# Last attention of a four-layer network: plain float32 products, a later turn of the probabilities, output tiles spread over units

## What is computed

```python
x = _rmsnorm(hidden_states, ln_w)
q = jnp.einsum('bqd,hd->bqh', x, wq).reshape(B, Qlen, N_HEADS, HEAD_DIM)
k = jnp.einsum('bkd,hd->bkh', encoder_hidden_states, wk).reshape(B, Klen, N_KV_HEADS, HEAD_DIM)
v = jnp.einsum('bkd,hd->bkh', encoder_hidden_states, wv).reshape(B, Klen, N_KV_HEADS, HEAD_DIM)
...
scores = jnp.einsum('bhqd,bhkd->bhqk', q, k) / np.sqrt(HEAD_DIM).astype(np.float32)
attn = jax.nn.softmax(scores.astype(jnp.float32), axis=-1).astype(q.dtype)
out = jnp.einsum('bhqk,bhkd->bhqd', attn, v)
return jnp.einsum('bqh,dh->bqd', out, wo)
```

## Time and profile before

| | |
|---|---|
| median of 3 runs | 1754.61 us (1748.97 to 1754.72) |
| profiled execution, its own time | 1750.64 us |
| span in the profile | 1748.9 us |
| busy: PE, PEld | 1451.7 us (83%), 1150.0 us (66%) |
| busy: DVE, ACT, POOL | 1115.7 us (64%), 461.4 us (26%), 312.8 us (18%) |
| chain that ended last, shares | PE 62%, DVE 26%, ACT 4%, issue 4%, DMA 2% |

### The profile page before, as it was taken

How to read it: one execution, slowest core, us unless ns; L and a number is a source line. 1 busy time by engine, 2 the same in 40 slices (tenths; PEclk the granted TensorE clock), 3 DMA queues, 4 the chain that set the end, 5 groups by cost and what they waited for, 6 DMA issues and landing times.

```text
span 1748.9 us, 19188 instructions
## 1 busy us (share of the span) xinstructions
PE 1451.7 (83%) x6585; PEld 1150.0 (66%) x6585; DVE 1115.7 (64%) x2569; ACT 461.4 (26%) x994; POOL 312.8 (18%) x186
## 2 busy tenths in 40 slices
PE   6559999998999889898377878589997566589998
PEld 5347776685776668686266767487886355477786
DVE  4567777768777658767967556634466788854142
ACT  3214423423334323232212113113213222122010
POOL 4101211211112112111121013116422421012120
PEclk9779999999999999899655897569998788799999
DMA  6421331322223221321011013001111000001011
GB/s 202 139 69 51 89 88 49 93 77 64 77 67 84 64 62 42 84 82 41 24 43 40 23 49 91 17 1 36 46 52 49 25 1 1 1 24 61 13 38 48
DMA packets 99409, 96.42 MB, mean 55 GB/s; under 512 B 13138, under 2 KB 72418, under 8 KB 99314
## 3 DMA queue, kind: packets, MB, share of 16 engines
q1 hardware_dynamic: 98802, 94.35, 18.3%
q0 software_dynamic: 512, 0.85, 0.2%
HBM read 84.34 MB, written 10.82 MB: 54 GB/s over the span
## 4 chain that ended last, share of the span: by engine, by line
PE 62%; DVE 26%; ACT 4%; issue 4%; DMA 2%; SPq 1%; POOL 1%; ACTq 0%; DVEq 0%; POOLq 0%
PE bank L1651 49%; PE bank L1991 5%; PE bank L1743 4%; DVE nf_y L1595 3%; DVE st L1136 2%; DVE xn L1154 1%; PE bank L1676 1%; DVE mx L1504 1%; DVE xT L1113 1%; DVE e L1518 1%; PE bank L1733 1%; DVE sm L1516 1%; DVE mx L1187 1%; PE bank L1947 1%; DMA nf_a<-in_L_w 1%
## 5 line engine op out<-in xcount | busy, mean ns | idle before, releaser
L1651 PE MATMUL bank<-xT,slots 128*128 128x512 f32 (+1 forms) x1920 | 471.2, 404 | 10.4 <-DVE xT L1113 6.9
L1651 PEld LDWEIGHTS bank<-xT,slots 128*128 128x128 f32 (+1 forms) x1920 | 357.1, 187 | 110.9 <-issue 10.2
L808 POOL TENSOR_TENSOR slots<-staging,slots 128x1024 fp32r<-128x1024 f32 (+4 forms) x97 | 230.2, 2376 | 1107.0 <-ACT slots L896 1106.9
L1595 DVE TENSOR_SCALAR nf_y<-nf_w 128x512 fp32r<-128x512 f32 (+2 forms) x495 | 233.6, 499 | 25.7 <-PE bank L1991 24.7
L1651 PE MATMUL bank<-slots,h 128*128 128x512 f32 (+1 forms) x728 | 181.7, 410 | 20.1 <-DVE h L1243 13.9
L1651 PEld LDWEIGHTS bank<-slots,h 128*128 128x128 f32 (+1 forms) x728 | 142.9, 197 | 56.8 <-DVE h L1243 14.8
L1991 PE MATMUL bank<-nf_y,nf_d 128*128 128x512 f32 (+2 forms) x495 | 169.7, 427 | 10.7 <-DVE nf_y L1595 8.5
L896 ACT ACTIVATE slots<-staging 128x1024 fp32r<-128x1024 f32 (+4 forms) x97 | 98.2, 1018 | 189.9 <-PE bank L1651 173.6
L929 ACT ACTIVATE e<-bank,mx 128x320 f32<-128x320 f32 x128 | 66.4, 524 | 272.2 <-DVE mx L1190 268.1
L1209 DVE TENSOR_TENSOR x<-bank,x 128x512 f32<-128x512 f32 x72 | 49.7, 690 | 125.7 <-PE bank L1651 125.6
L1991 PEld LDWEIGHTS bank<-nf_y,nf_d 128*128 128x128 f32 (+1 forms) x495 | 94.9, 197 | 46.9 <-issue 15.6
(11 more groups left out here) (244 smaller groups left out, 1905.0 us busy)
## 6 DMA issues: line engine op xcount, KB each, us to landing
staging<-in_L_wqkT SPq DMA_DIRECT2D x16, 480.0 KB, 3.7
nf_out<-nf_w SPq DMA_DIRECT2D x30, 256.0 KB, 2.1
staging<-nf_out SPq DMA_DIRECT2D x30, 256.0 KB, 2.8
staging<-in_L_woT SPq DMA_DIRECT2D x16, 384.0 KB, 3.3
staging<-in_L_w SPq DMA_DIRECT2D x12, 512.0 KB, 3.9
nf_a<-nf_max SPq DMA_DIRECT2D x40, 128.0 KB, 3.5
nf_r<-nf_rcp SPq DMA_DIRECT2D x40, 128.0 KB, 3.4
nf_w<-in_L_w SPq DMA_DIRECT2D x15, 256.0 KB, 4.2
```

Source lines behind the costliest of these rows:

```text
L808: g.tensor_tensor(lo, split_source(i), hi.bitcast(FP32), ALU.subtract).then_inc(*sig.mark("weight_low", i))
L1595: v.tensor_scalar(nf_y[0:rows, i % STAIR_RING, 0:size], w_, bound, first, compare, ALU.mult)\
L1651: ins = mm(dst, l_, r_, start=i == 0, stop=i == len(passes) - 1)
```

## The change

1. The inputs of the two products inside the last attention, q3, kr3, v3, kd3, vd3 and eT3, are kept once, in plain float32, and not as two parts. ScalarE copies the PSUM results with `keep`; the subtractions of VectorE for the keys, values, queries and turned probabilities are gone. `keys3` issues one product on GpSimd and `values3` two copies on VectorE.
2. `scores3` issues one plain product per tile on TensorE (before: three), `pv3` four (before: twelve).
3. `turn3` of a unit stands two iterations behind its scores and `pv3` three; e3 has three buffers. `values3` stands one iteration later, before the turn.
4. The result of `pv3` goes in two parts into a tile of its own, a3, with a place for two batches; `o3` reads it there.
5. In each of six iterations one output tile follows. `stats` (7,0) follows the fourth tile, and `turn` (7,0) stands two iterations behind it, inside the loop.

```diff
+TURN3_LAG, E3_RING = 2, 3
...
-    for n in range(len(units) + 2):
+    for n in range(len(units) + TURN3_LAG + 1):
         if n < len(units):
             steps.append(("scores3", n, *units[n]))
         if 1 <= n <= len(units):
             steps.append(("scale3", n - 1))
-        if n >= 2:
-            steps.append(("pv3", n - 2, *units[n - 2]))
-        if n < len(units):
-            steps.append(("values3", n, *units[n]))
+        if n > TURN3_LAG:
+            steps.append(("pv3", n - TURN3_LAG - 1, *units[n - TURN3_LAG - 1]))
         if 1 <= n <= len(units):
-            steps.append(("turn3", n - 1, *units[n - 1]))
-        if n >= 2:
-            if units[n - 2][1] == 0 and units[n - 2][0] >= 1:
-                steps += [("o3", TPB * (units[n - 2][0] - 1) + i) for i in range(TPB)]
-            if n - 2 == 3 * KT - 1:
+            steps.append(("values3", n - 1, *units[n - 1]))
+        if TURN3_LAG <= n < len(units) + TURN3_LAG:
+            steps.append(("turn3", n - TURN3_LAG, *units[n - TURN3_LAG]))
+        if n > TURN3_LAG:
+            b, c = units[n - TURN3_LAG - 1]
+            if b >= 1 and c < TPB:
+                steps.append(("o3", TPB * (b - 1) + c))
+            if (b, c) == (BPH, TPB - 1):
                 steps.append(("stats", 7, 0))
+            if (b, c) == (BPH, KT - 1):
+                steps.append(("turn", 7, 0))
         if n + 1 < len(units):
             steps.append(("keys3", n + 1, *units[n + 1]))
-    steps += [("turn", 7, 0)] + [("o3", TILES - 2), ("o3", TILES - 1), ("stats", 7, 1)]
+    steps += [("o3", TILES - 2), ("o3", TILES - 1), ("stats", 7, 1)]
...
-                for part in range(2):
-                    ins = g.tensor_tensor(kd3[:, n % 2, part],
-                                          kr3[:, part, c, b * CTX:(b + 1) * CTX].bitcast(FP32).unsqueeze(1).broadcast_to((P, HPC, CTX)),
-                                          hm3[:].unsqueeze(2).broadcast_to((P, HPC, CTX)), ALU.mult)
-                ins.then_inc(*sig.mark("keys3", n))
+                g.tensor_tensor(kd3[:, n % 2], kr3[:, c, b * CTX:(b + 1) * CTX].unsqueeze(1).broadcast_to((P, HPC, CTX)),
+                                hm3[:].unsqueeze(2).broadcast_to((P, HPC, CTX)), ALU.mult).then_inc(*sig.mark("keys3", n))
...
+            def keep(stage, key, dst, src):
+
+                act.wait_ge(*sig.when(f"{stage}_product", key))
+                sc.activation(dst, src, ACT.Copy).then_inc(*sig.mark(f"{stage}_kept", key))
...
-            def turn3(n, b, c):
-                for i in range(2):
-                    dve.wait_ge(*sig.when("turn3_high", (n, i)))
-                    v.tensor_tensor(eT3[:, 1, 2 * i:2 * i + 2], psum(("turn3", n, i))[:].rearrange("p (k n) -> p k n", k=2),
-                                    eT3[:, 0, 2 * i:2 * i + 2].bitcast(FP32), ALU.subtract)\
-                        .then_inc(*sig.mark("turn3_low", (n, i)))
...
-                    product(bank[:], [([q3[:, q, c, t * P:(t + 1) * P] for q in range(2)],
-                                       [kd3[:, n % 2, q].rearrange("p h k -> p (h k)") for q in range(2)])])\
+                    mm(bank[:], q3[:, c, t * P:(t + 1) * P], kd3[:, n % 2].rearrange("p h k -> p (h k)"), start=True, stop=True)\
                         .then_inc(*sig.mark("scores3_product", (n, i)))
...
-                pairs = [([vd3[:, n % 2, q, p] for q in range(2)], [eT3[:, q, p] for q in range(2)]) for p in range(PAIRS)]
-                product(bank[:, 0:S], pairs).then_inc(*sig.mark("pv3_product", n))
+                for p in range(PAIRS):
+                    ins = mm(bank[:, 0:S], vd3[:, n % 2, p], eT3[:, p], start=p == 0, stop=p == PAIRS - 1)
+                ins.then_inc(*sig.mark("pv3_product", n))
```

More of the change, by code:

```diff
@@ L300 @@
 SHARED = {f"{stage}_{kind}": f"{layer}_{kind}" for layer, stages in LAYER_STAGES.items() for stage in stages
-          for kind in ("product", "high", "low", "added")}
+          for kind in ("product", "high", "low", "added", "kept")}
 SHARED["h3_low"] = "layer3_low"
@@ L444, in build @@
         l = ExitStack()
[L445 to L451, removed]
+        q3 = sb("q3", [P, KT, TOK], FP32, l)
+        kd3 = sb("kd3", [P, 2, HPC, CTX], FP32, l)
+        vd3 = sb("vd3", [P, 2, PAIRS, P], FP32, l)
+        kr3 = sb("kr3", [P, KT, B * CTX], FP32, l)
+        v3 = sb("v3", [CTX, B, KV3 * HD3], FP32, l)
+        e3 = sb("e3", [P, E3_RING, TPB, HPC * CTX], FP32, l)
+        eT3 = sb("eT3", [P, PAIRS, S], FP32, l)
+        a3 = sb("a3", [P, 2, 2, KT, S], F32R, l)
         hm3 = sb("hm3", [P, HPC], FP32, l)
@@ L1487, in values3 @@
                 dve.wait_ge(*sig.when("vd3_clear", 0))
-                dve.wait_ge(*sig.when("v3_low", b))
+                dve.wait_ge(*sig.when("v3_kept", b))
                 groups = HPC // REP3
-                for part in range(2):
-                    src = v3[:, part, b, c * groups * HD3:(c + 1) * groups * HD3].bitcast(FP32)\
-                        .rearrange("p (u d) -> p u d", d=HD3).unsqueeze(2).broadcast_to((CTX, groups, PAIRS // groups, HD3))
-                    for j in range(2):
-                        blocks = vd3[CTX * j:CTX * (j + 1), n % 2, part].rearrange("p q (a d) -> p (q a) d", d=HD3)
-                        dst = blocks[:, j::HPC + 2].rearrange("p (u w) d -> p u w d", u=groups)
-                        ins = v.tensor_copy(dst, src)
+                src = v3[:, b, c * groups * HD3:(c + 1) * groups * HD3]\
+                    .rearrange("p (u d) -> p u d", d=HD3).unsqueeze(2).broadcast_to((CTX, groups, PAIRS // groups, HD3))
+                for j in range(2):
+                    blocks = vd3[CTX * j:CTX * (j + 1), n % 2].rearrange("p q (a d) -> p (q a) d", d=HD3)
+                    dst = blocks[:, j::HPC + 2].rearrange("p (u w) d -> p u w d", u=groups)
+                    ins = v.tensor_copy(dst, src)
                 ins.then_inc(*sig.mark("values3", n))
@@ L1931, in scores3 @@
             def scores3(n, b, c):
-                pe.wait_ge(*sig.when("q3_low", (c, b // BPH)))
+                pe.wait_ge(*sig.when("q3_kept", (c, b // BPH)))
                 pe.wait_ge(*sig.when("keys3", n))
@@ L1962, in o3 @@
                 bank = claim(("o3", t), ("o3_added", t))
-                pairs = [([q3[:, q, k, t * P:(t + 1) * P] for q in range(2)], [w[k // 2][q][:, k % 2] for q in range(2)])
+                b, i = divmod(t, TPB)
+                pairs = [([a3[:, b % 2, q, k, i * P:(i + 1) * P] for q in range(2)], [w[k // 2][q][:, k % 2] for q in range(2)])
                          for k in range(KT)]
```

53 lines of the change are left out of this document (21 added, 32 removed).

## The result

The change runs in 1711.43 us (median of 4 runs, 1706.19 to 1711.85), the kernel before beside it in 1754.66 us (4 runs, 1748.97 to 1759.38). The ratio is 0.9748, with a 95% interval of 0.9714 to 0.9783: some 43 us faster. On a second chip it was 0.9752 (0.9724 to 0.978; 1705.57 against 1751.44 us). The forecast was 1714 us.

What follows compares the result with a forecast made beforehand. VectorE was taken to bound the last attention (179 us). Savings and costs summed to -38.7 us, giving a 140 us stage, a profiled execution of 1711.9 us and a median of 1714 us; range 1699 to 1731.

Steps and rivals of the forecast that it cites:

- rests of turned probabilities and their wait: Last attention, VectorE: 32 rests (21.4 us) and 5.4 us waiting for ScalarE's copy go, all on the path: -26.8 us.
- copies of values: Last attention, VectorE: two copies in place of four, half of 15.1 us: -7.5 us.
- waits before additions in the loop: VectorE's idle time at three pairs of output tiles goes once single tiles are spread over iterations: -15.0 us.
- first keys: Start of the last attention: one key product on GpSimd suffices in place of two: -1.0 us.
- half-turn in the loop: `turn` (7,0) brings 4 VectorE subtractions into the loop, nothing given back for the tail: +2.6 us.
- meetings at the port: GpSimd's key products sometimes stop VectorE's multiplications or copies in the loop, about six hits: +6 us (0 to 16.5).
- plain products at start and end, small waits: TensorE's longer plain products, hidden in the loop, show at first scores, last values product and last scalings: +3 us (0 to 8).
- Rival B: Keys meet a multiplication in nearly each unit: +16.5 us in place of +6, 1725 us; chance 0.13.
- rival E: Later turn and third buffer remove nothing; the 5.4 us of waits stay: 1719 us, chance within the forecast's 0.60.
- A: TensorE becomes the bound in the last attention's loop, 159 us at clock 0.75: 1732 us; chance 0.10.
- D: Slower: TensorE bounds the loop and stays at the low clock; 199 us at 0.6, 1772 us; chance 0.04.
- C: No port meetings and a free tail, neither +6 nor +3, half-turn costs 1 less: 1704 us; chance 0.13.

Runs made afterwards that it cites:

- experiment 6: The change with the half-turn of the next normalisation moved back behind the last unit; 1708.4 us, ratio to before 0.9763.
- experiment 5: The change with GpSimd's key products made for the first two units only, reused by the other 14 (wrong attention); 1702.27 us, ratio to before 0.9727.
- Experiment 1: The change with one unit of lag and two buffers of e, everything else as changed; 1755.93 us, ratio to before 1.0047.
- experiments 2: The kernel before with only the output tiles spread, one per iteration instead of pairs; 1751.92 us, ratio to before 1.0003.
- experiment 7: The change with the first tile's scores product of each unit issued twice on TensorE; 1719.58 us, ratio to before 0.9832.
- experiment 3: The change with the output tiles in pairs again, everything else kept; 1712.93 us, ratio to before 0.9794.

## Why the prediction was right, and where it was not

The time came out within 3 us, and the terms of the sum mostly by themselves, each in the profile after:

| term | predicted, us | measured, us |
|---|---|---|
| rests of turned probabilities and their wait | -26.8 | -26.8 |
| copies of values | -7.5 | -6.6 |
| waits before additions in the loop | -15.0 | -14.8 |
| first keys | -1.0 | -1.0 |
| half-turn in the loop | +2.6 | +1.9 (experiment 6) |
| meetings at the port (what they add to the copies is in their line) | +6 | +2.6 |
| plain products at start and end, small waits | +3 | +2.8 (what is left) |

The last line is what is left of the stage's 41.9 us, and some of its parts can be seen: 0.4 us more from the first scores to the first maximum, 0.6 us of waits before later maxima, and 1.6 us more of waits before the rests of a (4.1 us; 2.5 before, there called q), all of them in the tail. The longer waits of the last two additions (5.4 us in place of 3.1) do not belong here: with the half-turn back in the tail they are 3.1 again (experiment 5). Of the 3.2 us between the sum, -38.7, and the stage, 2.5 are the port (3.4 less in its own line, 0.9 more in the copies') and 0.7 the half-turn. That the whole time came as near as 3 us is in part luck, since executions of one kernel scatter by more.

**Ports.** Measured gross, by experiment 5, the keys' meetings cost 5.2 us, half on multiplications and half on copies. Of these, 3.5 us lie above what the base of the sum already held (2.6 on multiplications, 0.9 that the copies did not save). The mechanism was right (multiplications and copies are held by a product of keys that wanders with TensorE), but six full hits beyond the old ones were too many. The Trainium skill, "SBUF — State Buffer", Who interferes with whom, gives the rule by which this is read: a VectorE instruction with at most one SBUF input does not contend unless it runs in a two-port mode, which copies can do. The traces agree: the rest of a and the maxima ran at 0.42 and 0.68 us beside a product of keys, as they do alone; copies and multiplications were held. Rival B, a meeting on the multiplication in each unit, did not come: 16 products at 1.03 would have been 16.5 us.

**Plain products.** The wide record was taken at 0.54 us, twice a narrow one. The weight loads of consecutive wide records in after stand 0.43 us apart at full clock:

```profile
1389.05 1.88 PE L1922 MATMUL bank<-kd,q 128*128 128x512 f32 x4
...
1389.48 0.19 PEld L1922 LDWEIGHTS bank<-kd,q 128*128 128x128 f32 x1 [0.24 <-issue]
...
1389.91 0.19 PEld L1922 LDWEIGHTS bank<-kd,q 128*128 128x128 f32 x1 [0.24 <-issue]
```

So a unit's scores take 1.88 us, not 2.2, its values product 1.99, not 2.2, its transposes 1.04, not 1.4 (the row it was taken from ran at a low clock), and TensorE needs 4.9 us of VectorE's 6.5, not 5.8. The Trainium skill, "FP8 and Floating Point Precision", TensorE Precision Notes, has true float32 as four passes. Four times the reduced record of 0.26 us is 1.03 us for a product of two records, an estimate of 2.1 us a unit. The trace agrees roughly: the estimate lies between the 2.2 taken and the 1.88 measured, and would hardly have changed the sum.

**The step that failed without hurting the sum** is the reading of what the lag does. The prediction gave it 5.4 us (rival E: without it 1719 us), and booked the tiles' 15 us under spreading. Experiment 1 puts the kernel without it at 1756 us, and experiments 2 and 3 put spreading at nothing, with either lag (the stage 2.4 us longer without the later turn, 0.6 with it). The sentence on which the 15 us rested, that a tile now follows a turn of probabilities scaled in the iteration before, is true of the lag, not of the spreading. And "VectorE is the bound of the loop, ... so all of it lies on the path" holds only with the lag. In the loop before, TensorE's way from the last multiplication through transposes to the next scores ran beside VectorE's rests and was nearly as long: with the 1.31 us of rests gone, a wait of 1.20 stands in their place (experiment 1). The total was right because all parts were in one change; that the 15 us came out under the wrong name is luck.

**Two readings that were wrong and cost nothing.** In an iteration with a tile the prediction gave TensorE 3.7 + 2.2 + 2.2 us and left out the transposes. Measured, TensorE has 3.06 for the tile, 1.88, 1.99 and 1.04, together 8.0 us against 7.65 of VectorE. It bounds nothing, since the scores are made ahead: those that began at 1418.56 were for the maximum at 1422.71. And ScalarE's copies of the turned probabilities are not two iterations away from who needs them, but one. TensorE idles 23.1 us in the loop for them; VectorE does not wait for the result. The group of after, in its loop:

```profile
L1940 PE MATMUL bank<-eT,vd 128*128 128x256 f32 x113 | 30.5, 415 | 23.1 <-ACT eT L893 23.1
```

**The other rivals.** A and D needed TensorE as the bound or a low clock: the loop has a granted clock of 0.90 (0.80 before), and experiment 7 put 13.8 us more on TensorE, and no maximum but the first waited longer. C, no meetings, is excluded by experiment 5. As to the marks: the quiet unit takes 6.51 us (6.6 said); no addition in the loop waits; VectorE is busy for 96% of the loop; a unit with a tile, from maximum to maximum, took 1422.71 - 1415.06 = 7.65 us (7.3 said), 0.52 of it a copy that was held; only the mark for the wide record is wrong. The term at start and end stood all the same, but no run separates its parts: besides the records, TensorE now has an output tile ahead of the last values products. In experiment 3, without that tile there, the tail is only 0.2 us shorter (12.9 us).

## What to carry to other kernels

Work that is taken off the bounding engine is gained only if no other engine's chain ran beside it: look at what the work covers, and ask how long the way out of the engine and back is (here multiplication, transposes, scores, maximum) against what the engine would still do meanwhile. If it is longer, lag the consumer by one more iteration first; here lag alone was worth 9 us, removal with the small moves -6, and both together 42. Where GpSimd and VectorE share a loop, place GpSimd's SBUF work under VectorE's instructions that read PSUM, and check what stands directly behind the point where it is released: released at the same point, it cost 4 us with copies behind that point and gained about 3 without them.

## What the runs showed of the hardware

The width of a plain float32 record follows the clock's two levels. The first scores of after ran in a stretch with a granted clock of 0.50, records some 0.85 us apart, the unit shown above from 1389 us in one of 1.00, at 0.43 us. The windows:

```profile
1366.50:1370.00 3.50, 2.48 (x3) 1.17 (x4) 0.40 (x1) 0.00 (x0) 1.92 (x2) 0.50 0.48 150
...
1389.00:1392.00 3.00, 1.93 (x6) 0.63 (x4) 2.90 (x6) 1.28 (x3) 0.92 (x1) 1.00 0.00 0
```

The timeline of after at the start of the stage, where the weight loads show it:

```profile
1367.52 4.79 PE L1922 MATMUL bank<-kd,q 128*128 128x512 f32 x6 [5.09 <-issue]
1368.51 0.33 PEld L1922 LDWEIGHTS bank<-kd,q 128*128 128x128 f32 x1 [0.52 <-issue]
1369.36 0.33 PEld L1922 LDWEIGHTS bank<-kd,q 128*128 128x128 f32 x1 [0.52 <-issue]
```

A copy of 64 x 64 elements, 0.19 us alone, is held by GpSimd just as a full multiplication is: two of them took 2.03 us, and the copies carried half of what the keys' meetings cost (2.7 of 5.2 us). And in one pair of profiles the two kernels reached the stage 5.3 us apart, 5.15 of them already at 632 us, where their code is the same: a stage's own bounds tell apart what the whole time, at four or five runs, does not.
